# Per-channel shifted 3x3 smoothing: fewer registers worked out ahead of a tile, and a narrower frame copy

## The reference

```
def _gn(v, G=32, eps=1e-5):
    g = v.reshape(B_, G, C_ // G, H_, W_)
    m = jnp.mean(g, axis=(2, 3, 4), keepdims=True)
    s = jnp.var(g, axis=(2, 3, 4), keepdims=True)
    return ((g - m) / jnp.sqrt(s + eps)).reshape(v.shape)
off_int = round(offset * SCALE); sub = offset * SCALE - off_int
shifted = x[:, ch, iy - dy, ix - dx], 0 outside the image
kern = jnp.exp(-(kx * kx + ky * ky) / (2.0 * SIGMA * SIGMA)); kern = kern / kern.sum()
out = depthwise 3x3 convolution of shifted with kern, padding 'SAME'
x = x + _L0_conv_ref(_gn(x), L0_conv_offset)
```

## Time and profile before

| | us |
|---|---|
| median of 3 runs | 973.79 |
| lowest and highest of them | 973.67 and 978.83 |
| the profiled execution, whole | 979.06 |
| its span, first to last instruction | 977.1 |
| bytes moved by the data queue | 402.71 MB |

### The profile page before, as it was taken

One profiled execution on the slowest core, in us unless ns is written; L12 is line 12 of the kernel. 1 busy time (PEld: TensorE's weight loads), 2 busy tenths in 40 slices (PEclk: granted clock), 3 DMA queues, 4 the chain that ended last, 5 costly groups with the idle time before them and its releaser, 6 DMA issues.

```text
span 977.1 us, 9088 instructions
## 1 busy us (share of the span) xinstructions
PE 785.6 (80%) x2132; PEld 383.6 (39%) x2132; DVE 824.8 (84%) x551; ACT 638.9 (65%) x461; POOL 368.1 (38%) x348
## 2 busy tenths in 40 slices
PE   0998987979979698897979879689797997979820
PEld 0544443434434343353434434345343443434410
DVE  7587988777798997978889899898998979797795
ACT  7778676564766747678466746577675785774661
POOL 0214034340432624013254393463845438250312
PEclk9999988989979799897998979989898897989955
DMA  9999999999999999999999999999999999999948
GB/s 364 427 401 423 392 405 429 429 429 428 430 429 430 432 428 414 430 429 430 431 429 406 398 433 376 407 419 393 431 408 430 430 427 431 431 431 430 430 208 343
DMA packets 27821, 403.09 MB, mean 413 GB/s; under 512 B 3216, under 2 KB 3216, under 8 KB 3216
## 3 DMA queue, kind: packets, MB, share of 16 engines
q1 hardware_dynamic: 27792, 402.71, 98.0%
HBM read 201.38 MB, written 201.33 MB: 412 GB/s over the span
## 4 chain that ended last, share of the span: by engine, by line
DVE 28%; DMA 27%; PE 20%; POOL 7%; issue 7%; ACT 5%; DVEq 3%; ACTq 2%; SPq 0%; POOLq 0%
PE sum_ps L289 17%; DMA out_dram<-xs 15%; DMA xs<-x_dram 12%; DVE xs L713 6%; DVE xs L716 6%; DVE smooth L709 6%; DVE smooth L704 6%; DVE xs L719 4%; POOL small L253 2%; POOL small L260 2%; ACT frame L417 2%; POOL small L257 2%; ACT unused L484 2%; POOL small L266 1%; ACTq L393 1%
## 5 line engine op out<-in xcount | busy, mean ns | idle before, releaser
L289 PE MATMUL sum_ps<-xs,bands 128*128 128x512 f32 x976 | 483.5, 653 | 51.2 <-DMA xs<-x_dram 51.2
L484 ACT ACTIVATE unused<-xs,small 128x4096 bf16 (+1 forms) x94 | 348.3, 3706 | 8.3 <-ACT small L470 4.8
L417 ACT ACTIVATE frame<-xs,small (+1 forms) x96 | 223.3, 2326 | 184.3 <-DVE smooth L709 183.3
L289 PEld LDWEIGHTS sum_ps<-xs,bands 128*128 128x128 f32 x976 | 200.6, 210 | 295.4 <-issue 282.2
L253 POOL TENSOR_TENSOR small<-small 128x3 f32<-128x3 f32 x32 | 41.6, 1299 | 570.6 <-ACT small L492 570.6
L289 PE MATMUL sum_ps<-xs,halves 128*128 128x512 f32 x496 | 230.0, 619 | 17.4 <-DMA xs<-x_dram 17.4
L704 DVE SCALAR_TENSOR_TENSOR smooth<-frame,side_w 128x612 f32 (+5 forms) x96 | 163.6, 1705 | 72.2 <-ACT frame L417 37.1
L713 DVE SCALAR_TENSOR_TENSOR xs<-smooth,small,xs 128x612 f32 (+5 forms) x96 | 163.5, 1703 | 51.9 <-POOL small L266 49.6
L709 DVE SCALAR_TENSOR_TENSOR smooth<-frame,side_w,smooth x96 | 159.7, 1664 | 7.5 <-DVE smooth L704 4.1
L719 DVE SCALAR_TENSOR_TENSOR xs<-smooth,small,xs 128x594 f32 (+9 forms) x96 | 159.8, 1664 | 3.4
L716 DVE SCALAR_TENSOR_TENSOR xs<-smooth,small,xs 128x594 f32 (+9 forms) x96 | 159.7, 1664 | 3.4
(11 more groups left out here) (132 smaller groups left out, 259.3 us busy)
## 6 DMA issues: line engine op xcount, KB each, us to landing
xs<-x_dram SPq DMA_DIRECT2D x96, 2048.0 KB, 14.8
out_dram<-xs SPq DMA_DIRECT2D x96, 2048.0 KB, 17.7
smooth<-offset_dram SPq DMA_DIRECT2D x1, 48.0 KB, 4.1
```

Source lines behind the costliest of these rows:

```text
L289: last = nc.tensor.matmul(sum_ps[:, :], (FIRST, SAME, SECOND)[i], slot_px(n, c * BANK, (c + 1) * BANK), start=(i == 0 and c == 0), stop=(i ...
L417: nc.scalar.activation(frame[:, bass.ds(b, rows * PITCH)].rearrange("p (r c) -> p r c", c=PITCH)[:, :, LEFT:LEFT + W], xs[:, bass.ds(a, ro ...
L484: nc.scalar.activation(unused[:, :], xs[:, bass.ds(n % SLOTS * PIX, PIX)], ACT.Square, bias=neg_mean[:, i:i + 1], accum_out=squares[:, i:i ...
```

## The change

On VectorE: the address beside the window becomes a fourth word in the table (`BESIDE`, in place of `COLUMN`), worked out once at the start. `tile_of` only moves the loop's count and names the registers; the parity and the address behind the window are worked out after the first pass is issued. The read of the next tile's four words moves from ahead of the second pass to behind it, ahead of the third. The column weights lie as `[P, 3, 6]` and are found by `done % 6` instead of a word. `base_w` keeps its three weights in the order centre, above, below. The loop runs from 1 to 96.

On ScalarE: a tile whose sideways shift is of kind 2 or 3 (window 34 or 18 columns) copies 34 columns, from column 0 or 30, and either all 64 rows or 34 of them. The word has a third field, and the tree has six leaves.

At the start: the chain of small VectorE operations gets thirteen in place of one ahead of `fills_ready`, and two more behind it. The words for ScalarE move into partitions 64 and up of the table `words`. GpSimd's six small writes of the column words go.

```diff
-            for i in range(2 * UT):
-                V.memset(word_of[:, :, COLUMN].rearrange("p (u i) -> p u i", i=2 * UT)[:, :, i], 3 * i)
...
-                    V.tensor_scalar(col_w[:, now * UT + i, :], base_w[:, position, :], rstd0[:, column],
+                    V.tensor_scalar(col_w[:, :, (now * UT + i + 1) % (2 * UT)], base_w[:, position, :], rstd0[:, column],
...
-                row = word & (1 << ROW_BITS) - 1
-                rows_kind = act.snap(word >> ROW_BITS)
+                column = word & (1 << COL_BITS) - 1
+                row = (word >> COL_BITS) & (1 << ROW_BITS) - 1
+                copy_kind = act.snap(word >> ROW_BITS + COL_BITS)
...
+                    rows, cols = COPIES[k]
...
-                choose(act, rows_kind, 0, len(SIDES), emit)
+                choose(act, copy_kind, 0, len(COPIES), emit)
...
-            chained(V.scalar_tensor_tensor(code[:, :, 0], kind[:, :, 1], float(1 << ROW_BITS), first_row[:, :, 1],
+            narrow, low, half = positive[:, :, 0], positive[:, :, 1], whole[:, :, 0]
+            chained(V.tensor_scalar(narrow, kind[:, :, 0], float(NARROW), None, ALU.is_ge))
+            chained(V.tensor_scalar(low, kind[:, :, 1], float(NARROW), float(len(SIDES)), ALU.is_ge, ALU.add))
+            chained(V.tensor_tensor(low, low, kind[:, :, 1], ALU.subtract))
+            chained(V.tensor_tensor(low, low, narrow, ALU.mult))
+            chained(V.tensor_tensor(low, low, kind[:, :, 1], ALU.add))
+            chained(V.tensor_scalar(half, kind[:, :, 1], float(NARROW), float(H - SIDES[NARROW]), ALU.is_ge, ALU.mult))
+            chained(V.tensor_scalar(half, half, float(H), None, ALU.subtract))
+            chained(V.tensor_tensor(half, half, narrow, ALU.mult))
+            chained(V.scalar_tensor_tensor(half, half, float(H), first_row[:, :, 1], ALU.add, ALU.min))
+            chained(V.scalar_tensor_tensor(code[:, :, 0], low, float(1 << ROW_BITS), half, ALU.mult, ALU.add))
+            chained(V.tensor_tensor(narrow, narrow, left, ALU.mult))
+            chained(V.tensor_scalar(narrow, narrow, float(W - SIDES[NARROW]), None, ALU.mult))
+            chained(V.scalar_tensor_tensor(code[:, :, 0], code[:, :, 0], float(1 << COL_BITS), narrow,
...
+            chained(V.tensor_tensor(code[:, :, 0], code[:, :, 0], side, ALU.subtract))
+            chained(V.tensor_scalar(by_tile(word_of[:, :, BESIDE]), for_halves(code[0:HALF, :, 0]),
...
                                        ).wait_op(tile_done, done_count, "sem-ge").then_inc(half_smooth, 1)
-
-                dve.reg_load(next_tile, words[0:1, bass.ds(done * WORDS, WORDS)])
-                V.scalar_tensor_tensor(part, frame_window(behind, cols - 1), side_w[1][:, bass.ds(n, 1)], part,
+                turn = kind_of % 2
+                behind = (src + 1 - turn).with_bounds(min_val=1, max_val=most + 1)
...
+                V.scalar_tensor_tensor(part, frame_window(behind, cols - 1), side_w[1][:, bass.ds(done, 1)], part,
                                        ALU.mult, ALU.add
                                        ).wait_op(half_smooth, done_count, "sem-ge").then_inc(smooth_ready, 1)
+
+                dve.reg_load(next_tile, words[0:1, bass.ds(done * WORDS, WORDS)])
                 dve.wait_ge(col_w_ready, done)
...
-            def tile_of(n):
-                dve.reg_mov(done_count, n + 1)
-                done = dve.snap(done_count, min_val=1, max_val=TILES)
+            def tile_of(done):
+                dve.reg_mov(done_count, done)
                 kind_of = dve.snap(next_tile[KIND], min_val=0, max_val=2 * len(SIDES) ** 2 - 1)
-                dve.reg_mov(at_turn, kind_of & 1)
-                turn = dve.snap(at_turn, min_val=0, max_val=1)
...
-                dve.reg_mov(at_behind, src + 1 - turn)
-                dve.reg_mov(at_beside, src + 2 * turn - 1)
-                beside = dve.snap(at_beside, min_val=0, max_val=FRAME_ROWS * PITCH)
-                behind = dve.snap(at_behind, min_val=0, max_val=FRAME_ROWS * PITCH)
-                weights = dve.snap(next_tile[COLUMN], min_val=0, max_val=(2 * UT - 1) * 3)
+                beside = dve.snap(next_tile[BESIDE], min_val=0, max_val=FRAME_ROWS * PITCH)
...
-            with dve.Fori(0, TILES) as n:
+            with dve.Fori(1, TILES + 1) as n:
```

More of the change, by code:

```diff
@@ L59, in build @@
     WORDS = 4
-    KIND, TO, FROM, COLUMN = range(WORDS)
+    KIND, TO, FROM, BESIDE = range(WORDS)
     ROW_BITS = (H - SIDES[-1]).bit_length()
+    NARROW = 2
+    COPIES = [(rows, W) for rows in SIDES] + [(SIDES[k], SIDES[NARROW]) for k in (0, NARROW)]
+    COL_BITS = (W - SIDES[NARROW]).bit_length()
     ctx = ExitStack()
@@ L93, in build @@
         rstd0, fix, rstd = (small[:, 18 + i * UT:18 + (i + 1) * UT] for i in range(3))
[L94 to L103, removed]
+        own_mean = small[:, 27:30]
+        own_sum = small[:, 30:31]
+        mean_64 = small[:, 31:33]
+        spread = small[:, 33:35]
+        last_sum = small[:, 35:36]
         base_w = xs[:, SLOTS * PIX:].rearrange("p (n k) -> p n k", k=3)
-        side_w = [sb(f"side_w{k}", [P, TILES]) for k in range(2)]
+        side_w = [sb(f"side_w{k}", [P, TILES + 1]) for k in range(2)]
         words = sb("words", [P, WORDS * (TILES + 1)], i32)
-        fills = sb("fills", [P, TILES], i32)
+        fills = words[HALF:P, 0:TILES]
         setup = smooth[:, 0:11 * 2 * POSITIONS].rearrange("p (n f a) -> p n f a", n=11, a=2)
@@ L667, in _ @@
             chained(V.tensor_tensor(tmp[:, :, 0], tmp[:, :, 0], norm[:, :, 1], ALU.mult))
-            for k in range(3):
-                last = V.tensor_tensor(base_w[:, :, k], e[:, k, :, 1], tmp[:, :, 0], ALU.mult)
+            for i, k in enumerate((1, 0, 2)):
+                last = V.tensor_tensor(base_w[:, :, i], e[:, k, :, 1], tmp[:, :, 0], ALU.mult)
             steps[0] += 1
@@ L680, in _, with smooth_tile @@
             V.engine_nop().then_inc(tile_done, 1)
-            next_tile = [dve.alloc_register(name) for name in ("next_kind", "next_to", "next_from", "next_column")]
+            next_tile = [dve.alloc_register(name) for name in
+                         ("next_kind", "next_to", "next_from", "next_beside")]
             done_count = dve.alloc_register("done_count")
-            at_turn, at_beside, at_behind = (dve.alloc_register(name) for name in ("turn", "beside", "behind"))
-            def smooth_tile(rows, cols, src, beside, behind, turn, dst, n, done, weights):
+            def smooth_tile(rows, cols, src, beside, kind_of, most, dst, done):
                 under = xs[:, bass.ds(dst, rows * W)]
@@ L700, in smooth_tile @@
                 sm = smooth[:, 0:rows * cols].rearrange("p (r c) -> p r c", c=cols)
-                part = smooth[:, bass.ds(turn, rows * cols)].rearrange("p (r c) -> p r c", c=cols)[:, :, 0:cols - 1]
                 dve.wait_ge(frame_ready, done)
-                V.scalar_tensor_tensor(sm, frame_window(beside, cols), side_w[0][:, bass.ds(n, 1)], frame_window(src, cols),
+                V.scalar_tensor_tensor(sm, frame_window(beside, cols), side_w[0][:, bass.ds(done, 1)], frame_window(src, cols),
@@ L741, in emit @@
                     smooth_tile(rows, cols, src.with_bounds(min_val=1, max_val=most),
-                                beside.with_bounds(min_val=0, max_val=most + 1),
-                                behind.with_bounds(min_val=1, max_val=most + 1), turn,
+                                beside.with_bounds(min_val=0, max_val=most + 1), kind_of, most,
                                 dst.with_bounds(min_val=0, max_val=(SLOTS - 1) * PIX + (H - rows) * W + W - cols),
-                                n, done, weights)
+                                done)
                 choose(dve, kind_of, 0, len(SIDES) ** 2, emit, 2)
```

54 lines of the change are left out of this document (30 added, 24 removed).

## The result

| | before | changed |
|---|---|---|
| median of 10 runs, us | 977.42 | 972.11 |
| lowest and highest | 973.67 and 978.88 | 969.70 and 974.25 |
| the profiled execution, us | 979.06 | 970.73 |
| its span, us | 977.1 | 968.7 |

The ratio of the changed kernel to the one before is 0.9954, with a 95% interval of 0.9942 to 0.9967. A second comparison gave 0.9958 (0.9944 to 0.9973). The kernel is faster by somewhat under half a per cent, and the interval lies across the line of 0.5%. Ten runs moved the median of before from 973.79 to 977.42: the three runs shown with it had held its two fastest.

What follows compares the result with a forecast made beforehand. Transfers were taken to bound most of the kernel, VectorE's lateness the middle losses. Middle -5.4 us, start +1 and end -1.2 gave -5.6 us, from 973.8 to 968.0 us with rounding; range 959.5 to 978 for 8 in 10.

Steps and rivals of the forecast that it cites:

- What bounds the kernel: Transfers at 430 GB/s bound most of it; VectorE's lateness sets the middle losses, some 19 us.
- The base: Time of the kernel before from which the difference is taken: 973.8 us, with about 14 us lost in the middle.
- The register work: VectorE's sequencer ahead of each tile's first pass: 0.4 us less per tile, 17 us of idleness over 43 gaps (0 to 23).
- The copies: ScalarE's narrow tiles: 40 us less copying, and 10 of VectorE's 37.1 us of copy waits gone (0 to 15).
- The sum: VectorE loses 27 us of idleness; only late runs count, so with start and end -5.6 us, 973.8 to 968.0.
- The read: Four-word read moved behind VectorE's second pass: its gap moves to L713, net 0 (-4 to +4 us).
- The start: Longer set-up chain: L677 2.2 us late, ScalarE's first means about 1.8, first units 1; cost +1 us (0 to +2.2).
- The end: Chain behind the last load: three tile boundaries at 0.3 to 0.45 us shorter, -1.2 us (0 to -1.6).
- Where the gain is given back: Late stretches: 3.5 of 7.4 us (532 to 620), 2.2 of 3.9 (620 to 732), 1.2 of 2.6, 0.4 of 5.5; 7.3 us.
- rival C: Slower: GpSimd weight operations miss the shorter gaps and are held a whole VectorE pass, 3.5 us; chance 0.12.
- Rival B: All lateness goes, copies also pulling each unit's weights ahead by 2 to 3 us: 959 to 963 us; chance 0.15.
- Rivals A and D: A: SyncE's load and store order absorbs the gain, 973.6, chance 0.25. D: edit saves neither registers nor copies, 976, chance 0.11.

Runs made afterwards that it cites:

- the mirror run: Four more compares and branches ahead of each tile's first VectorE pass, against the kernel before: ratio 1.0038 (1.0024 to 1.0052).
- The registers alone: The change without its narrow copies (ScalarE copies 64 columns as before), against the kernel before: ratio 0.9966 (0.9955 to 0.9977).
- the copies alone: Narrow copies with their word and 12 more set-up operations, VectorE's loop as before, against the kernel before: ratio 1.0016 (1.0002 to 1.0030).
- the longer chain: The kernel before with 14 more unused operations in VectorE's set-up chain: ratio 1.0022 (1.0008 to 1.0035).
- the two runs that took it away: VectorE's sum of tile 2 moved ahead of the set-up chain's end: in the changed kernel 0.9943, with narrow copies only 0.9987, both against the kernel before.

## Why the prediction was right or wrong

The step that failed is the base of the sum, 973.8 us for the typical execution of the kernel before: it measured 977.42. The difference set on it, -5.6 us, came out near: -5.3 us between the medians, -4.5 by the ratio. Part of that nearness is luck, since terms inside it erred to both sides, as told below.

**What bounds the kernel: right.** Transfers at 430 GB/s for most of it, and losses in the middle where VectorE is late. The gain is in 532 to 732 in both pairs of profiles, and in the 1.2 us of 364 to 532.

**The base: wrong, and it cost the most.** 968.0 us was forecast and 972.11 measured; 3.6 of the 4.1 us are the base. (The sum as written, 973.8 - 5.6, is 968.2; 968.0 is a rounding too far.) The prediction set its difference on the median of three runs, 973.79, though one of the three was at 978.83 and the profiled execution at 979.06. By bad luck the three held the two fastest of ten. Two of four executions near 979 should have put the base in the middle, near 976, and the supposition that the median execution is one that loses 5 us less rested on two runs. The same -5.6 us from 977.42 gives 971.8. Seen against the first base alone, 972.11 is a gain of 1.7 us, a third of what was forecast. The likeliest case, faster by over 0.5%, was given 0.50; the point lies at 0.46%, with the interval across that line.

**The register work: right that it is exposed, its size too low.** 0.4 us a tile was forecast. The groups fell by 0.37 us, but a boundary between tiles became 0.53 us shorter, because the forecast left out the small operation of L727 and the 30 ns or so beside every row. The visible gaps fell from 33.9 to 17.0 us against "about 17", and that agreement is luck: the 43 gaps gave up 21 us, and 4.2 us of new gaps came in where the copy used to be waited for. That this work is exposed at all was the step the forecast hung on, and the mirror run confirms it from the other side. The Trainium skill's queue depth (Advanced Engine Details and Errata, "Engine Queue Depths") would have given 0 by the prediction's reading of it, and the trace and both runs disagree with that use of it. The registers alone gave 3.3 us of the 4.5 us (0.0034 of 0.0046).

**The copies: right in ScalarE's time, wrong in their worth.** 40 us off ScalarE's busy time was forecast and 39.6 measured, so short rows cost nothing extra. The prediction added 17 and 10 us of idleness as if they were apart. They stand at the same place, ahead of the first pass, and the later one counts: the registers alone took 15.1 us off the two together, the copies alone 5.1, both 32.9. Take away only the copy and a gap is left, take away only the gap and some copies are waited for. With the registers as they were, 19.4 us went from the wait for copies and 14.3 us came back as gaps; with the registers gone too, the wait fell by 16 us instead of the 10 forecast.

**The sum: its 27 us of idleness failed too.** 32.9 us went ahead of the first pass, but 20.6 us came back at L743, and VectorE's whole idle time fell only from 152.3 to 141.1 us (149.1 to 144.0 in the second profiles). The time hardly suffered by that error, because the sum counted only what falls into late stretches. There, in 532 to 732, VectorE was busy for 3.8 us more (5.1 in the second pair), where the prediction took back 5.7 us.

**The read: right.** Net 0, with its 4 us moved to L743. That GpSimd's weights hide it in the first tile of a unit shows in neither profile apart.

**The start: right in place, too low in size.** L677 was expected near 22.5 us and started at 22.61; ScalarE's first means came 2.3 us late instead of 1.8. VectorE's first pass came 1.8 us late (30.48 to 32.28), where 1 us was forecast: the shorter copy gave its 0.85 us, but 0.39 us went to ScalarE's own register work ahead of it, which was put at 0.15 and as hidden. In time the late start cost 2.1 us in the longer chain, 1.5 and 2.8 us in the two runs that took it away, each with an interval of over 1 us to either side: some 2 us, where +1 (0 to +2.2) was forecast.

**The end: smaller than forecast.** The last two gaps fell by 0.53 us each. But from the landing of the last load to the end of the span it is 56.06 and 56.22 us before and 55.51 and 55.81 us after: some 0.5 us gained where 1.2 was forecast. The last 49 us have the same rate.

**Where the gain is given back.** The prediction expected 7.3 us back from the middle of the profiled execution and 5.4 of a typical one; the first pair of profiles gave 7.9, both together 5.1. What it did not foresee is what stands next: 20.6 of the 32.9 us of idleness taken away reappear at GpSimd's weights. The prediction's sign of rival C, the wait for weights grown by more than the gaps shrank, came true as worded: 20.6 us against 16.9. The kernel was faster all the same, since 16 us of copy waits had gone beside the gaps, and 532 to 732 lost less in both pairs, so C did not decide. Its mechanism, one more operation held for a whole pass, doesn't show either: operations of over 3 us on GpSimd number 30 and 28 before, 28 and 25 after. Those of over 1 us rose from 132 and 142 to 154 and 151, and GpSimd's busy time from 368.1 and 376.8 us to 389.3 and 384.0, so more of them were held for a part of a pass. How much of the 20.6 us is holding and how much is VectorE coming earlier stays open. Rival B named the unit's weights as what would have to move for more, and leaving out six GpSimd operations did give 4 us.

**Rivals A and D.** D fell with the first profile. A fell with the stretches: 394 and 403 to 411 and 410 GB/s, 415 and 414 to 425 and 424.

## What to carry to other kernels

When two things end at the same instruction, here the sequencer's register work and another engine's copy, their waits are not worth their sum one by one: taking one away uncovers the other, so price them together, place by place. Base a forecast of half a per cent on where all executions lie, the profiled one among them, not on the median of three. To size a small term, match the same boundary in two traces: here that repeated within 0.01 us while whole executions spread over 5 us, and it showed 0.53 us where a sum that happened to agree had said 0.4. And when an engine that is late is made faster, look for the wait that stands next in its tile, since most of the freed time may land there.

## What was not expected of the hardware

The chip hid none of about 2 us of register and branch work behind passes shorter than that. In all 96 tiles the sequencer's next row starts 12 to 14 ns after the start of the last pass, never before it, and the row that ends just ahead of the next tile's first pass ends 2.07 us later in the median, 1.53 us in the changed kernel. All 43 gaps of the kernel before stand behind last passes of 1.95 us or less.

A compare and branch costs more than its row: those added in the mirror run have rows of 43 ns in the median but start 74 ns apart, and four of them moved the next pass by 0.29 us.
